# A far path for three of four chunks, and VectorE copies for the near ones, in a graph-attention and FFN kernel

## What is computed

```python
# x: [6250, 256] f32; src, dst: 206250 edges, sorted by dst
def step(h, _):
    h = h + 0.01 * jnp.tanh(h)
    h = h * jax.nn.sigmoid(h)
    h = _layernorm(h, ln_w, ln_b)
    h = jnp.einsum('bsc,dc->bsd', h, W) + b
    return (h, None)

# attention: per edge e = leaky_relu(a_src[src] + a_dst[dst]), softmax over the
# edges of a node, weighted sum of h[src], + bias, relu
x = x + gat(layernorm(x), edge_index, W, att_src, att_dst, bias)
x = x + scan(step, layernorm(x), length=30)
```

## Time and profile before

| | |
|---|---|
| time, median of 3 runs | 4013.61 us (4010.14 to 4015.93) |
| the profiled execution | 4029.18 us, span 4027.3 us |
| busy in the span: TensorE matmul | 1552.1 us (39%) |
| VectorE | 3060.6 us (76%) |
| ScalarE | 2422.4 us (60%) |
| GpSimd | 2995.5 us (74%) |
| DMA | 720.44 MB, mean 179 GB/s |
| DMA issues: turned<-hs (L1211) | 444 of 256 KB |
| DMA issues: h2T<-turned (L1216) | 444 |

### The profile page before, as it was taken

How to read it: one execution, slowest core, us unless ns; L and a number is a source line. 1 busy time by engine, 2 the same in 40 slices (tenths; PEclk the granted TensorE clock), 3 DMA queues, 4 the chain that set the end, 5 groups by cost and what they waited for, 6 DMA issues and landing times.

```text
span 4027.3 us, 38921 instructions
## 1 busy us (share of the span) xinstructions
PE 1552.1 (39%) x7562; PEld 1333.1 (33%) x7562; DVE 3060.6 (76%) x7257; ACT 2422.4 (60%) x3681; POOL 2995.5 (74%) x2871
## 2 busy tenths in 40 slices
PE   3400000000000000000000001899999999999999
PEld 2300000000000000000000001788888888888877
DVE  7467586776775867758677586789988988888888
ACT  4334353443433434435334353689999999999987
POOL 7676676766766667667676673899998988998987
PEclk8755555555555555555555555999999999999999
DMA  7355565655655556556565564047777777777677
GB/s 200 113 177 193 179 213 172 211 190 166 218 186 187 202 165 218 180 181 220 166 213 195 176 213 141 22 117 183 187 183 186 182 178 178 175 177 173 175 184 182
DMA packets 646500, 720.44 MB, mean 179 GB/s; under 512 B 512713, under 2 KB 514794, under 8 KB 629862
## 3 DMA queue, kind: packets, MB, share of 16 engines
q1 hardware_dynamic: 560900, 486.61, 40.5%
q0 software_dynamic: 83824, 230.16, 19.9%
q10 hardware_dynamic: 1536, 1.18, 0.1%
HBM read 249.79 MB, written 352.38 MB: 150 GB/s over the span
## 4 chain that ended last, share of the span: by engine, by line
PE 22%; issue 21%; ACT 14%; POOL 11%; another core or an unknown queue 11%; DVE 10%; DMA 10%; SPq 2%; DVEq 0%; ACTq 0%; POOLq 0%
PE ps L1663 18%; ACT G L639 8%; POOL G L732 8%; DVE RS L968 4%; DMA turned<-hs 3%; DVE psum L949 2%; DMA sums<-G 2%; DMA h2T<-turned 2%; PE ps L1649 2%; POOL h L1288 2%; DMA G<-haug,idx 2%; SPq L1216 1%; ACT hs L1385 1%; ACT th L1396 1%
## 5 line engine op out<-in xcount | busy, mean ns | idle before, releaser
L732 POOL DMA_INDIRECT G<-haug,idx x1612 | 1524.7, 946 | 739.7 <-issue 491.8
L1663 PE MATMUL ps<-WT,h2T 128*128 128x256 f32 x5880 | 1341.2, 382 | 22.7 <-DMA h2T<-turned 22.0
L1663 PEld LDWEIGHTS ps<-WT,h2T 128*128 128x128 f32 x5880 | 1095.6, 191 | 176.4 <-DMA h2T<-turned 38.9
L968 DVE TENSOR_TENSOR_SCAN RS<-keep,psum 128x845 f32<-128x845 f32 x496 | 940.5, 1899 | 185.2 <-remote 115.9
L1288 POOL TENSOR_TENSOR h<-Hs,th 128x512 f32<-128x512 f32 (+1 forms) x750 | 934.6, 1257 | 136.1 <-ACT th L1396 130.9
L1053 PE MATMUL psum<-AD,ones 128*128 128x512 f32 x2 | 2.1, 1141 | 2298.6 <-DVE AD L1070 2298.6
L631 ACT ACTIVATE decay<-el,ZC 128x4 f32<-128x4 f32 x124 | 37.1, 299 | 1298.1 <-remote 521.3
L639 ACT ACTIVATE G<-RS 128x845 f32<-128x845 f32 x496 | 781.9, 1723 | 39.0 <-DVE RS L968 37.0
L1573 DVE SCALAR_TENSOR_TENSOR Hs<-ps,rs,b 128x256 f32<-128x256 f32 x1470 | 676.4, 460 | 145.3 <-PE ps L1663 131.7
L1053 PEld LDWEIGHTS psum<-AD,ones 128*128 128x128 f32 x2 | 0.5, 310 | 2298.9 <-DVE AD L1070 2298.9
L1555 DVE BATCH_NORM_STATS2 cst<-h 128x6 f32<-128x256 f32 x1470 | 546.9, 413 | 42.3 <-ACT h L1373 41.1
(11 more groups left out here) (164 smaller groups left out, 1196.5 us busy)
## 6 DMA issues: line engine op xcount, KB each, us to landing
sums<-G SPq DMA_DIRECT2D x124, 1716.0 KB
turned<-hs SPq DMA_DIRECT2D x444, 256.0 KB
G<-haug,idx POOLq DMA_INDIRECT x1612
h2T<-turned SPq DMA_TRANSPOSE x444
haug<-G SPq DMA_DIRECT2D x7, 924.0 KB
X<-x SPq DMA_DIRECT2D x7, 784.0 KB
own<-haug SPq DMA_DIRECT2D x5, 924.0 KB, 4.8
adz<-G SPq DMA_DIRECT2D x4, 830.5 KB
```

Of the source, the lines that this page charges most:

```text
L732: pool.indirect_dma_start(out=G[:, u, t, :], out_offset=None, in_=haug[:, :], in_offset=bass.IndirectOffsetOnAxis(ap=idx[:, i % 2, u * T + ...
L968: v.tensor_tensor_scan(RS[:, k % 2, h, :, :].rearrange("p f t -> p (f t)"), keep[:, k % 2, :, :].rearrange("p f t -> p (f t)"), ps_m[:, h, ...
L1663: last = nc.tensor.matmul(ps_g[q.u][:, a * C:(a + 1) * C], h2T[:, q.u, (a * 2 + k) * P:(a * 2 + k + 1) * P], WT[:, k, :], start=(k == 0), ...
```

## The change

From pass 54 on a pass is near when q % 4 == 3 (or the chunk is the short one) in place of q % 3 == 2. There are then 492 far passes and 258 near ones, where there were 444 and 306. The near passes from 54 on are copied out of PSUM by VectorE, in step p after the second `affine` for pass p+2, with the same two waits as the copy on ScalarE had; ScalarE's copies end with pass 53. TensorE's waits for a copy go against a new semaphore, `s_copied`, for those passes. `s_own` becomes two semaphores, one a slot, that count up, in place of one a part.

```diff
+NEAR = 4
-FAR = [q >= FAR0 and q % 3 != 2 and j != NC - 1 for q, j in enumerate(ORDER)]
+FAR = [q >= FAR0 and q % NEAR != NEAR - 1 and j != NC - 1 for q, j in enumerate(ORDER)]
...
-        s_own = [sem(f"s_own{b}") for b in range(NF)]
+        s_own = [sem(f"s_own{n}") for n in range(2)]
+        s_copied = sem("s_copied")
...
+        def wait_copies(pe, nears):
+
+            early = NEARS[FAR0 - 1]
+            if nears > early:
+                pe.wait_ge(s_copied, nears - early)
+            elif nears > 0:
+                pe.wait_ge(s_h2T, nears)
...
# ScalarE, step p
                 q = p.on(-3)
-                if 4 <= q.n < ALL and not q.far:
+                if 4 <= q.n < FAR0:
                     copy_t(q)
...
# VectorE
+            def copy_t(q):
+                n = q.w * C
+                dve.wait_ge(s_xp, NEARS[q.n])
+                wait_count(dve, s_prod, q.n + 1 - RX)
+                v.tensor_copy(h2T[:, q.u, 0:n], ps_x[q.x][:, 0:n]).then_inc(s_copied, 1)
...
# VectorE, step p
                     affine(lag, 1)
+                q = p.on(2)
+                if FAR0 <= q.n < ALL and not q.far:
+                    copy_t(q)
...
# TensorE, transposes and product
-                wait_count(pe, s_h2T, NEARS[q.n] - 2)
+                wait_copies(pe, NEARS[q.n] - 2)
...
-                    pe.wait_ge(s_h2T, NEARS[q.n])
+                    wait_copies(pe, NEARS[q.n])
```

More of the change, by code:

```diff
@@ L1205, in own_rows @@
                 t0, t1 = FT[b:b + 2]
-                sp.dma_start(own[:, b % 2, 0:t1 - t0, :], haug.rearrange("(p i) c -> p i c", i=NT)[:, t0:t1, :]).then_inc(s_own[b], 16)
+                sp.dma_start(own[:, b % 2, 0:t1 - t0, :], haug.rearrange("(p i) c -> p i c", i=NT)[:, t0:t1, :]).then_inc(s_own[b % 2], 16)
             def send(q):
@@ L1277, in own_tile @@
                 if i == 0:
-                    pool.wait_ge(s_own[b], 16)
+                    pool.wait_ge(s_own[b % 2], 16 * (b // 2 + 1))
                     pool.wait_ge(s_part, b + 1)
@@ L1337, in own_tile @@
                 if i == 0:
-                    act.wait_ge(s_own[b], 16)
+                    act.wait_ge(s_own[b % 2], 16 * (b // 2 + 1))
                     act.wait_ge(s_part, b + 1)
@@ L1519, in all_weighted @@
                 ch.add(gathered(b, 0, n))
-                dve.wait_ge(s_own[b], 16)
+                dve.wait_ge(s_own[b % 2], 16 * (b // 2 + 1))
                 own_rows(b, OWN_ACT[b], n).then_inc(s_scaled, 1)
```

## The result

The changed kernel takes 4097.02 us (median of 6 runs, 4075.24 to 4101.18), the kernel before, run beside it, 4011.37. The ratio is 1.0204, with a 95% interval of 1.0186 to 1.0222: 82 us slower (the two medians are 86 apart). The forecast was 4031, 18 us slower, within 3999 to 4060. The sign came, at more than four times the size.

The account below looks back on a forecast made before the run. TensorE was taken as the late bound, with several engines nearly full early and SyncE's landings deciding the sign. Early +21, late -3, elsewhere 0 gave +18 us on the median of 4013.6: 4031, range 3999 to 4060.

Parts of the forecast that it names:

- The signs it named: Early stretch: SyncE's waits for ScalarE far below 135.6 us in 600, for landed writes above 78; product waits more for DMA.
- The early pace: Stretch before short chunks come every tenth pass: 2.05 to 2.08 us a pass, where it was 2.010.
- Step 5, SyncE's series: SyncE's queue: three far chunks hold two write landings (L, issue to landing) in series, 8.26 us per four passes; +21 early.
- several queues full at once: Rival, chance 0.13: L near its mean or lengthened by load, VectorE without room; over +35 us, 4049 to 4070.
- Late stretch: Passes with short chunks: SyncE 1.79 us a pass against 1.813 before; up to 6 us gained, 3 taken.
- Step 1: TensorE loses transposes of 48 full near chunks, 21 us; floor falls to 1.915 us a pass early, 1.77 late.
- Step 2: ScalarE loses 252 copies and gains 48 splits: 90 us less busy time, some 0.13 us a pass.
- Step 3: VectorE gains 204 PSUM copies, 0.6 us per 128x512; hidden at 1.97 us a pass early; at 0.9 us, 28 us lost.
- Step 4: The waits of VectorE's copy cost nothing, since what it waits for is already done.
- Step 6: DMA engines carry 9/8 of the far chunks, busy 0.84 early, not full; nothing added to L, the risk kept in the range.

Follow-up runs that it names:

- e11: The changed kernel with one more SyncE wait: turn 1 of a run of three far chunks waits until write 2 has landed; ratio to the kernel before 1.0634.
- e1: The kernel before with only the far pattern changed to q % 4 != 3, copies left on ScalarE; ratio to the kernel before 1.0229.
- e3: The changed kernel with SyncE issuing all sends of a run of far chunks first, then their turns; ratio to the kernel before 0.9982.
- e0: The changed kernel unaltered, timed again on the chip of a follow-up set; ratio to the kernel before 1.0224.
- e6: The changed kernel with the sends issued by ScalarE, so that SyncE only waits and turns; ratio to the kernel before 0.9990.

## Why the prediction was wrong

The mechanism and the sign were right; the size was off in one term, SyncE's series. The signs it named came: SyncE's waits for ScalarE fell to 11.9 us, its waits for landed writes rose from 78.0 us in 600 to 226.1 in 700, and the weight loads' waits for `h2T` from 13.1 to 103.5. The early pace, 2.184 us a pass, is beyond the 2.05 to 2.08 named.

**Step 5, SyncE's series, is the step that failed.** It took 2 x (L + 1.34) with L = 2.79, the median of seven landings, for both writes: 8.26 us; the runs of three measured 8.74. Two errors of like size are in it. A queue without slack adds up its landings, so the mean counts: the first landing's mean was 2.94, close to the 2.91 that the step named and passed over, which gives 8.50, +23 us in 380 passes more. And the second landing was taken to be like the first. It is slower, 3.10 against 2.94 (in the medians 2.97 against 2.58), and e11 shows the reason: turn 1 is issued behind it and its transfer runs beside it. In the order of before no write stands between two turns. That and what is left of the first make 8.74, another +23. From the forecast's +21 early these two lead to the measured 66.

One of the seven landings was misread as well. In the group sent at 2762.10 the second send ends at 2764.89 and the turn starts at 2764.98: SyncE was held by ScalarE's split, not by the write. Without that 2.88 the median is 2.74 and the mean 2.92, so it moves the mean by nothing.

**The case "several queues full at once"** named the right point, an L of about 2.9, and put +35 us or more on it, up to 4070; 4097 lies above even that. It got 0.13, though the mean of the step's own seven rows was 2.91. Its other part, VectorE without room, did not matter: e1 has the same loss without the copies.

**Late stretch.** -3 was forecast, +4 to +8 came (1.827 for 1.813 by the windows, 546.4 us for 538.7 by the passes), and 5.5 us behind it, where nothing was forecast. With 8.7 for a group of three, step 5's own sum makes (3 x 8.7 + 2 x 5.47)/20 = 1.85 us a pass in place of 1.79, somewhat above the 1.827 measured. SyncE still waits 32.4 us for ScalarE in the late 400, so it is near its limit there, not all the time at it. That is argued from the two, and no run isolates it.

**Step 1, TensorE.** 972 transposes, as said. Its saving of 21 us does not reach the time: with three of four far and SyncE out of the way the best is 0.9982, 7 us. In e3 TensorE's busy time is 582.8/301 = 1.94 us a pass, near the floor of 1.915; what keeps the pace at 1.99 is mostly its 16.4 us of waits for far chunks. Which of the steps ahead of those chunks makes them late is not settled; holding the turns back is one candidate, the full ScalarE another.

**Step 2, ScalarE.** 492 splits and 54 copies, as said. Moving the copies is worth 1% where SyncE is out of the way (0.9982 against 1.0088), and buys nothing in the change.

**Step 3, the copy.** 0.679 us for 128x512, inside 0.5 to 0.896; it lasts 0.08 longer than the 0.6 taken for its share of the engine. The step's "VectorE hides it" held in the change: the far pattern costs the same with or without it. Its 28 us for a copy of 0.9 us counts the whole 0.075 us a pass, although 0.04 of it would still have fitted between 1.97 and 2.010; nothing hung on it. The estimate by the Trainium skill's "VectorE: DVE Perf Modes", section on the TRN2 errata, was 0.66 us; the row of 0.679 agrees within some 3%, better than for L1573.

**Step 4, the waits.** The copies waited for nothing, as said: the idle time ahead of them is 0.0.

**Step 6, the DMA engines.** They were not the limit: 207 GB/s in e3. But leaving L untouched was the second half of the error above. The rule of the Trainium skill's "DMA: Bandwidth & Descriptors", section "Latency and other measured facts", that the fixed cost grows under load, pointed the right way: the write with another transfer beside it takes 0.4 us longer. The runs show that for one particular transfer; whether landings grow with load in general none of them isolates. e3 moves more bytes a second than the change without loss, but with one landing in series instead of two.

## What to carry to other kernels

A queue that waits for its own transfers is a resource like an engine: write its program out in order, count how many landings stand in series in one period, and compare that with the period before changing how often it is used; sends first, then the waits for them, costs one landing where interleaving costs two. Add up means and not medians when a stage will have no slack, since nothing repairs a late landing any more. And when an engine shows a large wait for a buffer, follow it back before adding buffers: here the fourth buffer moved part of the wait and left the pace.

## What the hardware showed beyond that

A write of 256 KB to device memory landed after 3.11 us on average with a transposing read issued just behind it and one just ahead of it (e0, 69 runs), and after 2.70 with only the one ahead (e11, 61 runs). A DMA issued by ScalarE reads 0.34 us on its queue and costs the engine hardly more than nothing: from 2400 to 3000 us in e6 the `tanh` starts 0.58 us after the `silu` ahead of it where an issue lies between (204 times), and 0.53 where none does (69).
